# Attention and experts of one layer: the first half's output projection between keys and values, VectorE's delta steps in another order, and the first rows' transposes behind the last scores

## The reference, cut to what matters

```
q = layernorm(x) @ Wq.T + bq;  k, v = ctx @ Wk.T + bk, ctx @ Wv.T + bv
scores = clip(q k / 4, -50, 50), -50 where the key is masked;  probs = softmax(scores)
delta = clip_scale(probs v @ Wo.T + bo)              # residual scale, non-finite values replaced
delta = layernorm(delta) * gamma + beta
x = x + tanh(g_xattn) * delta
hs = layernorm(x);  logits = hs @ router.T;  probs = softmax(logits);  top 2 of 8, renormalised
out = sum over the two experts of weight * ((up * silu(gate)) @ down),  up, gate = hs @ gate_up[e]
x = x + tanh(g_ffn) * out
```

## Time and profile before

| what | value |
|---|---|
| timed runs | 274.09, 277.58, 277.39 us, median 277.39 us |
| profiled execution, its own time | 274.56 us |
| its span, from the first to the last instruction | 272.9 us |
| granted TensorE clock, mean | 0.925 |
| TensorE busy | 229.1 us (84%) |
| VectorE, ScalarE, GpSimd busy | 176.3, 138.4, 56.2 us |

### The profile page before, as it was taken

One profiled execution on the slowest core, in us unless ns is written; L12 is line 12 of the kernel. 1 busy time (PEld: TensorE's weight loads), 2 busy tenths in 40 slices (PEclk: granted clock), 3 DMA queues, 4 the chain that ended last, 5 costly groups with the idle time before them and its releaser, 6 DMA issues.

```text
span 272.9 us, 7014 instructions
## 1 busy us (share of the span) xinstructions
PE 229.1 (84%) x2708; PEld 175.9 (64%) x2708; DVE 176.3 (65%) x422; ACT 138.4 (51%) x220; POOL 56.2 (21%) x90
## 2 busy tenths in 40 slices
PE   0879996219999999999999387999997829999994
PEld 0667785208888888888888276966664416556663
DVE  2788549701456998677659985692999850573535
ACT  3745769911555789699757632343334517101010
POOL 2470000200155332100002211033444643000000
PEclk9999999557999999999999959599999975999999
DMA  7999204660871589996991000310000002000002
GB/s 223 327 417 386 76 21 116 208 269 4 293 276 40 182 324 324 396 355 177 390 419 60 4 2 2 54 20 0 0 0 2 1 0 67 0 0 2 0 0 67
DMA packets 12868, 37.54 MB, mean 138 GB/s; under 512 B 2320, under 2 KB 10016, under 8 KB 10528
## 3 DMA queue, kind: packets, MB, share of 16 engines
q1 hardware_dynamic: 11728, 36.13, 37.1%
q10 hardware_dynamic: 1008, 0.92, 1.3%
q0 software_dynamic: 96, 0.00, 0.0%
HBM read 35.14 MB, written 0.92 MB: 132 GB/s over the span
## 4 chain that ended last, share of the span: by engine, by line
PE 66%; DVE 12%; issue 11%; DMA 3%; POOL 3%; ACT 3%; SPq 1%; DVEq 0%; POOLq 0%; ACTq 0%
PE bank L803 13%; PE bank L537 11%; PE bank L544 10%; PE bank L565 6%; PE bank L554 6%; PE bank L820 6%; PE bank L792 4%; DMA x_sb<-x_dram 3%; POOL x_sb L514 3%; PE bank L697 2%; PE bank L683 2%; PE bank L529 2%; PE bank L522 1%; PE bank L673 1%; DVE p L1147 1%
## 5 line engine op out<-in xcount | busy, mean ns | idle before, releaser
L537 PE MATMUL bank<-ctx_pair,wk 128*128 128x250 f32 x152 | 40.4, 409 | 17.6 <-issue 10.0
L906 ACT ACTIVATE p<-bank,mask_bias,mask_scale 125x896 f32<-125x896 f32 x38 | 39.7, 1095 | 27.8 <-PE bank L554 27.8
L803 PE MATMUL bank<-rowsT,gate_up 128*128 128x448 f32 x112 | 46.0, 557 | 0.0
L537 PEld LDWEIGHTS bank<-ctx_pair,wk 128*128 128x128 f32 x152 | 29.2, 202 | 23.2 <-issue 18.4
L544 PE MATMUL bank<-wv,ctx_pair 128*125 128x256 f32 x152 | 36.4, 383 | 0.0
L1147 DVE TENSOR_SCALAR p<-p 125x912 f32<-125x912 f32 x38 | 27.6, 738 | 12.1 <-ACT p L906 12.1
L803 PEld LDWEIGHTS bank<-rowsT,gate_up 128*128 128x128 f32 x112 | 21.9, 197 | 17.9 <-issue 17.2
L544 PEld LDWEIGHTS bank<-wv,ctx_pair 128*125 128x125 f32 x152 | 28.8, 190 | 4.4
L1029 ACT ACTIVATE silu<-bank 128x448 f32<-128x448 f32 x16 | 8.7, 546 | 44.9 <-PE bank L803 41.6
L820 PE MATMUL bank<-down,act 128*112 128x256 f32 x128 | 30.3, 380 | 1.3 <-DVE act L1455 1.3
L820 PEld LDWEIGHTS bank<-down,act 128*112 128x112 f32 x128 | 22.4, 177 | 9.4 <-issue 3.7
(11 more groups left out here) (163 smaller groups left out, 316.7 us busy)
## 6 DMA issues: line engine op xcount, KB each, us to landing
ctx_all<-ctx_dram SPq DMA_DIRECT2D x13, 1500.0 KB, 8.7
ctx_pair<-ctx_dram SPq DMA_DIRECT2D x38, 125.0 KB, 5.2
gate_up<-ctx_dram SPq DMA_DIRECT2D x3, 1500.0 KB, 10.9
gate_up<-gate_up_dram SPq DMA_DIRECT2D x1, 2048.0 KB, 12.8
down<-down_dram SPq DMA_DIRECT2D x1, 1024.0 KB, 14.8
num<-acc SPq DMA_DIRECT2D x16, 57.0 KB, 2.3
x_sb<-x_dram SPq DMA_DIRECT2D x2, 448.0 KB, 6.2
out_dram<-x_sb SPq DMA_DIRECT2D x4, 224.0 KB, 2.3
```

Of the source, the lines that this page charges most:

```text
L537: mm = nc.tensor.matmul(bank[:, K_BANK, 2 * TT * m:2 * TT * (m + 1)], wk[:, k, P * m:P * (m + 1)], tile[:, :, k, :], start=(k == 0), stop= ...
L803: mm = nc.tensor.matmul(bank[:, GU_BANK[s % 2] + g, 0:HR], gate_up[:, e, k, g, :], rowsT[:, k, HR * h:HR * (h + 1)], start=(k == 0), stop= ...
L906: nc.scalar.activation(p_tile[:, t].rearrange("t (j n) s -> t j n s", j=4)[:, :, :, 0:S], bank[0:TT, 0:4, DEN * t:DEN * (t + 1)].rearrange ...
```

## The change

On TensorE, `pair_kv` is split into `pair_k` and `pair_v`; for pairs 15 and 16 the output projection of (0, 0) and (0, 1) now stands between keys and values, where it stood behind the values. The transposes of (0, 0) now stand behind the scores of pair 17, where they stood ahead of them. On VectorE, `delta_parts(0, 0)` goes ahead of the copy of values 15 and `add_gains(0, 0)` ahead of that of values 16; `h_offsets(0, 0)` goes ahead of the copy of values 17, and `delta_parts(0, 1)`, which stood ahead of it, now comes behind that copy and the sums of pair 15. The sums of pair 16 come ahead of the clips of pair 17. Behind the loop come `delta_whole` of (0, 1), the sums of pair 17, and only then `add_gains(0, 1)`, `add_delta(0, 1)` and `h_offsets(0, 1)`. ScalarE's, GpSimd's and SyncE's programs are as before.

```diff
--- before.py
+++ after.py
@@ -568,11 +568,12 @@
                                               stop=True, skip_group_check=True)
                 mm.then_inc(semaphore, 1)
 
-            def pair_kv(i):
-
+            def pair_k(i):
                 pe.wait_ge(pair_in[i % RING], 32 * (i // RING + 1))
                 after(pe, main.k_out, i)
                 k_proj(ctx_pair[i % RING], main.k_mm)
+
+            def pair_v(i):
                 after(pe, main.v_out, i)
                 if i == 15:
                     pe.wait_ge(wide_out, 1)
@@ -647,7 +648,8 @@
             def early_pairs(i):
 
                 with pe.If(tiles > 2 * (LAST - i)):
-                    pair_kv(i)
+                    pair_k(i)
+                    pair_v(i)
                     if i >= 2:
                         pair_pv(i - 2)
                     pair_scores(i)
@@ -767,19 +769,22 @@
             for i in range(NOPT):
                 early_pairs(i)
             for i in range(NOPT, NTAIL):
-                pair_kv(i)
+                pair_k(i)
+                if i == 15:
+                    pe.wait_ge(wide_out, 1)
+                if i in (15, 16):
+                    project_out(0, i - 15)
+                pair_v(i)
                 if i == 11:
                     pe.wait_ge(q_raw_out, 4)
                     masked_sums(0)
                 if i == 14:
                     use("spread0")
                     spread_inverse(0, 0, misc(0, 2 * DEN)).then_inc(misc_mm, 1)
-                if i in (15, 16):
-                    project_out(0, i - 15)
                 pair_pv(i - 2)
+                pair_scores(i)
                 if i == 17:
                     h_transposes(0, 0)
-                pair_scores(i)
                 if i == 14:
                     pe.wait_ge(main.v_out, 15)
                     spread_inverse(0, 1, bank[:, V_BANK]).then_inc(wide_mm, 1)
@@ -1232,10 +1237,6 @@
                 dve.wait_ge(wide_mm, 1)
                 flat = tot[:, 1].rearrange("p b s -> p (b s)")
                 nc.vector.tensor_tensor(flat, flat, bank[:, V_BANK, 0:2 * DEN], ALU.mult).then_inc(wide_out, 1)
-
-            def delta_of(h, n):
-                delta_parts(h, n)
-                delta_whole()
 
             def delta_parts(h, n):
 
@@ -1419,6 +1420,10 @@
             for i in range(NOPT):
                 early_pairs(i)
             for i in range(NOPT, NTAIL):
+                if i == 15:
+                    delta_parts(0, 0)
+                if i == 16:
+                    add_gains(0, 0)
                 v_copy(main, v[i % VRING], i + 1)
                 if i == 14:
                     totals(0)
@@ -1432,18 +1437,15 @@
                 if i == 14:
                     wide_mix()
                 if i == 15:
-                    delta_of(0, 0)
+                    delta_whole()
                 if i == 16:
-                    add_gains(0, 0)
                     add_delta(0, 0)
+                if i == 17:
+                    delta_parts(0, 1)
+                    pair_sums(16)
                 clips(main, p[i % 2], 2 * i + 1)
                 if i == 16:
-                    delta_parts(0, 1)
                     h_offsets(0, 0)
-                    delta_whole()
-                if i == 17:
-                    add_gains(0, 1)
-                    add_delta(0, 1)
                 if i < 12:
                     sum_all(*DVE_SUMS[i - 4])
                 if i == 11:
@@ -1465,10 +1467,12 @@
                     nc.vector.scalar_tensor_tensor(x_sb[:, r], out, weight[:, r, e:e + 1], x_sb[:, r], ALU.mult,
                                                    ALU.add).then_inc(d_out, 1)
 
-            pair_sums(NTAIL - 2)
+            delta_whole()
+            pair_sums(NTAIL - 1)
+            add_gains(0, 1)
+            add_delta(0, 1)
+            masked_sums(1)
             h_offsets(0, 1)
-            pair_sums(NTAIL - 1)
-            masked_sums(1)
             shift_logits(0)
             expert_ranks(0)
             expert_weights(0)
```

## The result

| | before | changed |
|---|---|---|
| median of 8 timed runs | 277.49 us | 280.43 us |
| lowest to highest | 274.09 to 278.95 us | 279.05 to 281.43 us |
| span of the profiled execution | 272.9 us | 277.6 us |

The ratio is 1.0127, with a 95% interval of 1.0083 to 1.0171: the change costs 1.3%. The forecast was 278.1 us in a range of 273.9 to 282.4; sign and range held, and the size was larger than the sum gave (2.1 us; the medians differ by 2.9, the profiled executions' spans by 4.7).

A forecast was written before the change was run, and what follows sets the result against it. TensorE, busy 84% of the span, was taken as the bound, through its waits and low clock. -2.5 + 3.8 + 0.8 = +2.1 us on 276.0, the middle of four executions, gave 278.1 us, range 273.9 to 282.4.

The forecast's parts named there:

- (a): Projection between keys and values, pairs 15 and 16: same TensorE instructions, costed at nothing, bounds 0 to 0.3 us.
- (b): VectorE's steps for (0, 0): `fix_raw` near 136.7 us, guess near 143.5, 2.0 us earlier, offsets at 152.7 instead of 155.21.
- (c): Transposes of (0, 0): start at 155.0 instead of 156.49 us, held by `MISC_BANK`; TensorE's wait cut from 4.31 to some 1.7.
- (d): Up to the first halves of experts 0 and 1: they start at 158.5 instead of 161.07 us, 2.5 us won.
- (e): Loop's end on VectorE: gains of (0, 1) queue behind sums of pair 17; 2.5 us won become 1.3 us lost.
- slow clock at the first halves: Rival, chance 0.20: halves take up to 6.0 us, sums of pair 17 come 2.8 us later; +5.8 in all, 281.8 us.
- (f): Clock behind the wait: low stretch may reach expert 0's output and expert 2's input; 0.8 us, bounds 0 and 1.9.
- no loss: Rival, chance 0.20: full clock at router and second halves gives back 1.1 + 0.3 of the 1.3 us; 276.0 us.
- (g): `pack(1)` starts at 163.5 instead of 167.98 us, behind the sums of pair 17; costed at nothing.
- a gain by `pack(1)`: Rival, chance 0.15: `pack(1)` starts 4.5 us earlier and up to 4.5 us come back in the second half; 273.6 us.

The follow-up runs named there:

- e1_sums_behind: Changed kernel with the sums of pair 17 moved behind the gains and residual of (0, 1) on VectorE; 275.80 us, ratio 0.9971 to the kernel before.
- e2_tail_alone: Kernel before with only the gains and residual of (0, 1) moved out of the loop, behind the sums of pair 17; 281.63 us, ratio 1.0213.
- e9_three_waits_filled: Changed kernel with `delta_whole` in the loop, sums of pair 17 behind the offsets of (0, 1), and unread matmuls in three waits; 273.87 us, ratio 0.9880.
- e6_and_filled_second: e5_whole_in_loop with 10 unread matmuls ahead of the transposes of (1, 1), in the second half's longest wait; 274.51 us, ratio 0.9878 to the kernel before.
- e5_whole_in_loop: Changed kernel with `delta_whole` of (0, 1) right behind `delta_parts`, and the sums of pair 17 behind gains and residual; 275.92 us, ratio 0.9955 to the kernel before.
- e4_filled_wait: Changed kernel with 12 unread matmuls between the masked sums and the transposes of (0, 1); 279.08 us, ratio 1.0083 to the kernel before.

## Why the prediction was right, and where its sum was off

**(a), (b), right.** Keys 15 to keys 17 take 14.68 us in both kernels, so (a) costs nothing. The positions of (b) came within 0.5 us, and 0.44 of that is the later start of the stretch: `fix_raw` at 137.05 (forecast 136.7), guess at 143.86 (143.5), offsets from 152.27 (151.9).

**(c), right.** The transposes of (0, 0) started at 155.31 (155.0) after 1.62 us of waiting (1.7), and they waited for the read of `MISC_BANK`, not for the rows.

**(d), right.** Halves at 158.93 (158.5); counted from keys 17, 2.6 us won (2.5).

**(e), right in mechanism, mis-sized.** The wait of 6 us at the transposes of (0, 1) is there (5.95), behind the sums of pair 17; e1_sums_behind cuts it to 3.40 and brings the transposes back to where they were before, and e2_tail_alone makes the same wait (5.94). The term was put at 3.8 us (from 2.5 won to 1.3 lost) and measured 5.6 (from 2.6 won to 3.0 lost). The step that was mis-sized is "At the full clock the product ends at 162.6": the halves took 4.91 us, not 3.2, because the clock was at half from about 155.4 to 162.3 us. The product ended at 164.77, of which 0.4 is the later start of the stretch, and this reaches the transposes one to one: without the 1.7 us the loss would be the forecast's 1.3. The first rival, slow clock at the first halves, had priced up to 2.8 us more; it came about by 1.7 of them. I gave it 0.20, although had the halves of the kernel before at 0.50. In every profiled execution but that of e9_three_waits_filled, which filled the two waits, the clock fell to half between 155.1 and 158.7 us; in e2_tail_alone it fell at 155.1 and was back when the halves began.

**(f), wrong in place, near in size by luck.** I took 0.8 us, in expert 0's output, and said that the router and second halves already paid the half clock before. It was 1.3 us, and it is the router (3.16 instead of 2.23) and the transposes (0.98 instead of 0.60): in the kernel before the clock fell only at 171.1 us, in the middle of the router, and its 2.23 us in the earlier trace rows should have told me. Expert 0's output took 1.89 us as before. The price in the rival "no loss" was off too: at 1.00 a router of the same shape took 1.74 us (e9_three_waits_filled), 0.5 less than 2.23, not 1.1.

**(g), right.** `pack(1)` started at 165.75 instead of 168.00, and nothing came of it: the rest of the span is 94.7 us against 94.8, and the second half's wait for the rows of (1, 1) is 4.94 us as before. The rivals "no loss" and "a gain by `pack(1)`" are out.

**The sum.** -2.6 + 5.6 + 1.3 makes +4.4 before rounding (34.87 - 30.51) from keys 17 to the output, against the forecast's -2.5 + 3.8 + 0.8 = +2.1. The sum was made for the profiled execution, and there it is 2.3 us short. That the median moved by only 2.9, nearer to 2.1, is luck: it fits with the spread of the kernel before, whose profiled execution was near its fastest. The forecast's 278.1 was also reckoned from the middle of four executions, 276.0, while the median of eight is 277.49.

**What I had not seen.** The part of (e) that isn't the sums: with them moved away (e1_sums_behind) the transposes of (0, 1) come no sooner than in the kernel before (21.25 against 21.24), although the halves start 2.9 us sooner. `delta_whole` stood behind the clips of pair 17; with it in the loop as well they come at 20.24 (e6_and_filled_second), unless the halves are slow, since the offsets then still wait for TensorE (21.29, e5_whole_in_loop). With the offsets ahead too they come at 19.75, with halves of 4.87 us and of 3.27 us alike.

## What to carry to other kernels

When a wait is made shorter at the front, follow what is queued on the helping engine behind the next thing that it waits for: here one pair of additions, put ahead of a chain on VectorE, made the next rows 3.0 us late together with a slow clock (e1_sums_behind took that back), more than the 2.6 us won in front; and even without it the rest of the chain had to be moved before anything of the gain was left. On an in-order engine, steps whose inputs are ready go ahead of steps that wait for the bottleneck engine, unless the bottleneck waits for those first. And price a stretch of TensorE between two waits at both clock levels.

## What the runs showed of the hardware

The first halves, sixteen instructions that are the same in all kernels, took 3.26 and 3.27 us in windows at a granted clock of 1.00 (e2_tail_alone, e9_three_waits_filled), 6.04 and 6.30 us at 0.50 for all but the last 0.4 us or less (e5_whole_in_loop, e4_filled_wait), and 4.7 to 5.1 us where the clock came back on the way. The page "TensorE: Matmul & The Clock Gate" of the Trainium skill, section "Part 1: The HAM clock gate (the "warmup" mystery)", says that the moment of a change differs from run to run; 6.04 us in e5_whole_in_loop and 4.95 us in e6_and_filled_second, whose programs are the same up to there, agree. The router took 3.15 us at 0.50 and 1.74 us at 1.00, and the clock fell inside it in e4_filled_wait and e6_and_filled_second although TensorE had hardly waited before it (0.69 and 0.62 us; 0.64 and 0.62 us): filling a wait doesn't by itself protect what follows. The page's section "Why this matters for your kernels" names long gaps between bursts of matmuls as what brings the clock down; these two falls, and that at 155.4 us in the changed kernel behind a wait of 1.62 us, came behind short ones, and the measurement decides.
